# Three small edits to a fused attention and expert kernel: circuits mixed on TensorE, biases as bf16 parts, inverse norms as a power on GpSimd

## The reference

```python
q, k, v = split(query @ W_qkv.T + b_qkv)         # 8 heads of 16
encode(x) = x / max(sqrt(sum(x * x)), 1e-12) * exp(1j * phases)
q_ent, k_ent = entangle(encode(q)), entangle(encode(k))   # three depths
for c in range(4):                               # circuits
    scores = abs(pattern(q_ent, k_ent)) ** 2 * gain[c]    # 8 x 8 per token
    amps = sqrt(softmax(scores) + 1e-12)
    co = (amps @ vq) * coherence_phase
    final += sup_w[c] * clip(abs(co), 1e-6, 1.0) * sign(co)
attention = real(final) @ W_out.T + b_out
```

## Time and profile before

| | us |
|---|---|
| three runs of the kernel before | 1626.47, 1627.81 (median), 1628.41 |
| the profiled execution | 1626.89 |
| its span, from first to last instruction | 1624.8 |
| PE busy | 1261.8 (78%) |
| DVE busy | 1286.0 (79%) |
| ACT busy | 789.0 (49%) |
| POOL busy | 720.2 (44%) |

### The profile page before, as it was taken

One profiled execution on the slowest core, in us unless ns is written; L12 is line 12 of the kernel. 1 busy time (PEld: TensorE's weight loads), 2 busy tenths in 40 slices (PEclk: granted clock), 3 DMA queues, 4 the chain that ended last, 5 costly groups with the idle time before them and its releaser, 6 DMA issues.

```text
span 1624.8 us, 20010 instructions
## 1 busy us (share of the span) xinstructions
PE 1261.8 (78%) x6269; PEld 948.2 (58%) x6269; DVE 1286.0 (79%) x1606; ACT 789.0 (49%) x1605; POOL 720.2 (44%) x579
## 2 busy tenths in 40 slices
PE   4568988698987988698598988877888887988241
PEld 2345766667675666666377675746657574756131
DVE  6558788988969888888768898896788879888653
ACT  4337445545545554645436464543546465543110
POOL 1261423274534353475534352466625343435654
PEclk9989989889889979989788998979889899989575
DMA  7423321424323241523215141331515142331101
GB/s 210 132 71 96 100 80 55 125 72 118 101 61 105 63 134 52 164 72 116 74 49 163 40 149 48 100 99 57 169 36 157 39 135 76 97 82 34 33 20 45
DMA packets 110670, 147.27 MB, mean 91 GB/s; under 512 B 14921, under 2 KB 84198, under 8 KB 110054
## 3 DMA queue, kind: packets, MB, share of 16 engines
q1 hardware_dynamic: 101350, 125.01, 25.5%
q0 software_dynamic: 8192, 16.79, 3.3%
q10 hardware_dynamic: 1024, 4.20, 2.0%
HBM read 113.81 MB, written 32.13 MB: 90 GB/s over the span
## 4 chain that ended last, share of the span: by engine, by line
PE 47%; DVE 19%; ACT 13%; issue 11%; POOL 8%; DMA 1%; SPq 0%; ACTq 0%; POOLq 0%; DVEq 0%
PE ps_t L720 6%; PE ps_r L760 6%; PE ps_q L720 6%; PE ps_r L761 5%; PE ps_h L643 5%; PE ps_f L651 4%; DVE pat L1630 4%; POOL rows_in L1246 3%; DVE u_sgn L1704 3%; POOL got L1259 2%; DVE prod L1601 2%; PE ps_k L707 2%; PE ps_f L653 2%; ACT u_sgn L1066 2%; ACT hid L1085 2%
## 5 line engine op out<-in xcount | busy, mean ns | idle before, releaser
L1224 POOL TENSOR_TENSOR prod<-expo,vT 128x512 f32<-128x512 f32 x192 | 237.1, 1265 | 426.7 <-ACT expo L1048 265.1
L1216 POOL TENSOR_TENSOR prod<-kq 128x1024 f32<-128x1024 f32 x64 | 149.7, 2360 | 276.9 <-ACT kq L1020 276.9
L643 PE MATMUL ps_h<-turned,w_tile 128*128 128x128 f32 x1248 | 186.5, 296 | 65.8 <-ACT turned L1078 54.1
L643 PEld LDWEIGHTS ps_h<-turned,w_tile 128*128 128x128 f32 x1248 | 166.6, 204 | 109.0 <-ACT turned L1078 86.5
L1606 DVE TENSOR_TENSOR prod<-expo,ps_v 128x2048 f32<-128x2048 f32 x80 | 181.2, 2285 | 58.0 <-PE ps_t L720 35.2
L1630 DVE TENSOR_REDUCE pat<-prod 128x128 f32<-128x2048 f32 x96 | 218.7, 2280 | 9.7 <-POOL prod L1216 8.0
L1085 ACT ACTIVATE hid<-ps_h,w_tile 128x128 f32<-128x128 f32 x624 | 178.0, 368 | 64.8 <-PE ps_h L643 63.8
L1601 DVE TENSOR_TENSOR prod<-ps_q,kq 128x1024 f32<-128x1024 f32 x128 | 150.5, 1217 | 72.5 <-ACT kq L1020 59.0
L760 PE MATMUL ps_r<-sqx,mats 128*128 128x512 f32 x256 | 165.2, 732 | 49.7 <-ACT sqy L1000 31.6
L651 PE MATMUL ps_f<-w_tile,hid 128*128 128x128 f32 x1248 | 174.8, 286 | 2.3 <-ACT turned L1078 2.3
L1246 POOL DMA_INDIRECT rows_in<-xn,row_of x128 | 126.4, 987 | 87.9 <-DVE tile_expert L1590 50.1
(11 more groups left out here) (262 smaller groups left out, 2286.8 us busy)
## 6 DMA issues: line engine op xcount, KB each, us to landing
w_tile<-w_cat SPq DMA_DIRECT2D x156, 514.0 KB
x_tile<-rows_in SPq DMA_DIRECT2D x156, 64.0 KB
rows_out<-turned SPq DMA_DIRECT2D x156, 64.0 KB
rows_in<-u SPq DMA_DIRECT2D x2, 2496.0 KB, 11.7
yacc<-in_L_attn_query_dram SPq DMA_DIRECT2D x16, 256.0 KB, 4.0
out_dram<-yacc SPq DMA_DIRECT2D x16, 256.0 KB, 2.9
x_sb<-in_L_attn_query_dram SPq DMA_DIRECT2D x11, 256.0 KB, 4.0
b_tile<-in_L_ffn_b_dram SPq DMA_DIRECT2D x156, 0.5 KB
```

Of the source, the lines that this page charges most:

```text
L643: last = nc.tensor.matmul(ps_h[:, c, :], w_tile[:, n % WS, c * P:(c + 1) * P], turned[:, x_turn(n) % FS, 0, :], start=True, stop=True)
L1224: last = pool.tensor_tensor(dst[:, at], w[:, at], v[:, at], ALU.mult)
```

## The change

PE mixes the circuits: `clip_and_mix` ends with one product `u * u_sgn` over all 2048 values, and a new `mix_circuits` sums the four circuits with four f32 products by diagonal matrices that hold the weights. The sum lies in PSUM (`ps_t`), where `measure` reads it, so `sum_circuits` and `msum` go. `mix_circuits(o)` stands between `q_operands(k, 2)` and the tile before `control_tiles(n)`; in a routed step the wait for the routing's read of `ps_t` (`rank_read`) moves there with it. POOL inverts the norms in a new `invert_norms(n)`, the first call of its step: a lower limit and a power of -0.5. Both biases become three bf16 parts added in one pass: `b_out` through the 96-row product that `b_qkv` has, `b2` through a three-row product whose rows SP loads with each tile from a small table in DRAM.

```diff
-                sp.dma_start(b2_tile[:, n % WS, :], b2[bass.ds(e, 1), :]).then_inc(w_landed.of(n), 16)
+                sp.dma_start(b2_tile[:, n % WS, :], b2_parts[bass.ds(e, 1), :, :].rearrange("e r c -> (e r) c")).then_inc(w_landed.of(n), 16)
...
+            sp.wait_ge(bias_split, 12)
+            for part in range(3):
+                sp.dma_start(b2_parts[:, part, :], b_parts[32 * part:32 * part + E, QKV + C:QKV + 2 * C]).then_inc(cat_made, 16)
...
-                nc.tensor.matmul(ps_f[:, 1, :], ones[0:1, :], b2_tile[:, n % WS, :], start=False, stop=True).then_inc(turn_psum.sem, 1)
+                nc.tensor.matmul(ps_f[:, 1, :], ones_parts[:], b2_tile[:, n % WS, :], start=False, stop=True).then_inc(turn_psum.sem, 1)
...
+            def mix_circuits(k):
+                pe.wait_ge(mix_ready.sem, mix_ready.value(k))
+                for c in range(NC):
+                    last = nc.tensor.matmul(ps_t.rearrange("p (t c) -> p t c", t=T), sup_mats[:, c, :], u[:, :, c, :],
+                                            start=(c == 0), stop=(c == NC - 1))
+                last.then_inc(msum_psum.sem, 1)
...
-                    last = nc.tensor.matmul(ps_t[:, at], ones[0:1, :], b_out_row[:], start=False, stop=True)
+                    last = nc.tensor.matmul(ps_t[:, at], pick[:], b_parts[:, QKV:QKV + C], start=False, stop=True)
...
-            def norm_sqrt(k):
-                act.wait_ge(ss_step.sem, ss_step.value(k))
...
-                act.activation(norm[:], ss[:, 1, :], ACT.Sqrt).then_inc(norm_ready.sem, 1)
...
-            def sum_circuits(k):
...
-                    tt(msum[:], u_sgn[:, :, 0, :] if c == 1 else msum[:], u_sgn[:, :, c, :], ALU.add, msum_step)
+            def invert_norms(k):
+                pool.wait_ge(ss_summed.sem, ss_summed.value(k))
+                pool.tensor_scalar(ss[:, 1, :], ss[:, 0, :], 1e-24, None, ALU.max).then_inc(ss_clamped.sem, 1)
+                pool.wait_ge(ss_clamped.sem, ss_clamped.value(k))
                 if k >= 1:
-                    pool.wait_ge(meas_ready.sem, meas_ready.value(k - 1))
...
+                    pool.wait_ge(v_ready.sem, v_ready.value(k - 1))
+                tt(rnorm[:], ss[:, 1, :], minus_half[:], ALU.pow, rnorm_ready)
...
+                for c in range(NC):
+                    const(dve.tensor_scalar(sup_mats[:, c, :], ident[:], sup[:, c:c + 1], None, ALU.mult))
...
             def normalise(k):
-                dve.wait_ge(norm_ready.sem, norm_ready.value(k))
-                dve.tensor_scalar(rnorm[:], norm[:], 1e-12, None, ALU.max).then_inc(rnorm_step.sem, 1)
-                dve.wait_ge(rnorm_step.sem, rnorm_step.value(k, 1))
-                dve.reciprocal(rnorm[:], rnorm[:]).then_inc(rnorm_step.sem, 1)
-                dve.wait_ge(rnorm_step.sem, rnorm_step.value(k))
+                dve.wait_ge(rnorm_ready.sem, rnorm_ready.value(k))
...
-                for c in range(NC):
-                    dve.scalar_tensor_tensor(u_sgn[:, :, c, :], u[:, :, c, :], sup[:, c:c + 1], u_sgn[:, :, c, :],
-                                             ALU.mult, ALU.mult).then_inc(mix_ready.sem, 1)
+                tt(u[:], u[:], u_sgn[:], ALU.mult, mix_ready)
```

More of the change, by code:

```diff
@@ L179, in build @@
         w_gate = sb("w_gate", [P, E])
-        b_parts = sb("b_parts", [96, QKV], BF16)
+        b_parts = sb("b_parts", [96, QKV + 2 * C], BF16)
+        ones_parts = sb("ones_parts", [3, P], BF16)
         pick = sb("pick", [96, P], BF16)
@@ L219, in build @@
         ss = sb("ss", [P, 2, T * 3 * NH])
-        norm = sb("norm", [P, T * 3 * NH])
+        minus_half = sb("minus_half", [P, T * 3 * NH])
         rnorm = sb("rnorm", [P, T * 3 * NH])
@@ L346, in build @@
         sq_ready = signal("sq_ready", T)
-        ss_step = signal("ss_step", 2)
-        norm_ready = signal("norm_ready")
-        rnorm_step = signal("rnorm_step", 2)
+        ss_summed = signal("ss_summed")
+        ss_clamped = signal("ss_clamped")
+        rnorm_ready = signal("rnorm_ready")
         a0_ready = signal("a0_ready")
@@ L707, in project @@
                     nc.tensor.matmul(p_cols, xnT[:, k % XN, t * P:(t + 1) * P], w_proj[:], start=True, stop=False)
-                    nc.tensor.matmul(p_cols, pick[:], b_parts[:], start=False, stop=True).then_inc(proj_psum.sem, 1)
+                    nc.tensor.matmul(p_cols, pick[:], b_parts[:, 0:QKV], start=False, stop=True).then_inc(proj_psum.sem, 1)
             def sums(k, unit):
@@ L844, in _ @@
                     q_operands(k, 2)
+                if exists(o):
+                    if routed is not None:
+                        pe.wait_ge(rank_read.sem, rank_read.value(routed))
+                    mix_circuits(o)
                 tiles(k, 3, 4)
@@ L851, in _ @@
                 if exists(o):
-                    if routed is not None:
-                        pe.wait_ge(rank_read.sem, rank_read.value(routed))
                     turn_m(o)
@@ L1055, in abs_sign @@
                 if k >= 1:
-                    act.wait_ge(msum_step.sem, msum_step.value(k - 1))
+                    act.wait_ge(msum_psum.sem, msum_psum.value(k - 1))
                 else:
@@ L1195, in _ @@
             split(pool.memset(pick[:], 0.0))
+            split(pool.memset(ones_parts[:], 1.0))
             for row in (0, 32, 64):
                 split(pool.memset(pick[row:row + 1, :], 1.0))
-            pool.wait_ge(bias_in, 48)
+            split(pool.memset(minus_half[:], -0.5))
+            pool.wait_ge(bias_in, 80)
             split(pool.tensor_copy(b_parts[:], b_in))
@@ L1623, in sums @@
                     if k >= 1:
-                        dve.wait_ge(mix_ready.sem, mix_ready.value(k - 1))
+                        dve.wait_ge(msum_psum.sem, msum_psum.value(k - 1))
                     else:
@@ L1702, in clip_and_mix @@
                 dve.wait_ge(clip_ready.sem, clip_ready.value(k))
-                for c in range(NC):
-                    dve.scalar_tensor_tensor(u_sgn[:, :, c, :], u[:, :, c, :], sup[:, c:c + 1], u_sgn[:, :, c, :],
-                                             ALU.mult, ALU.mult).then_inc(mix_ready.sem, 1)
+                tt(u[:], u[:], u_sgn[:], ALU.mult, mix_ready)
             def measure(k):
-                dve.wait_ge(msum_step.sem, msum_step.value(k))
+                dve.wait_ge(msum_psum.sem, msum_psum.value(k))
                 dve.wait_ge(phase_ready.sem, phase_ready.value(k))
```

41 lines of the change are left out of this document (16 added, 25 removed).

## The result

The changed kernel takes 1702.9 us (median of 4 runs, 1697.4 to 1705.4) against 1628.1 us for the kernel before: a ratio of 1.0447, with a 95% interval from 1.0408 to 1.0485. That is 4.5% slower, where the prediction had 1577 us and a chance of 0.08 for slower. The profiled execution took 1697.4 us, its span 1695.7.

The account below looks back on a forecast made before the run. It took PE and DVE, handing work back and forth with neither full, to bound the kernel. Its terms, 24 + 5 + 2 - 5 + 6 + 2 + 16 = 50 us, took 1626.9 to 1577 us, range 1540 to 1610.

Parts of the forecast that it names:

- the price of the power: POOL's power of -0.5 on 96 values, at the head of its step: between 0.22 and 4.5 us, taken as 2 us.
- The rival that named the power: POOL's power is long: past 10 us each microsecond delays 15 steps, 1727 us at a 20 us power; chance 0.08.
- the room: At the head of POOL's step, read in block 7's step: the power may take about 10 us and cost nothing.
- the likeliest case: The forecast itself, 1577 us, with its own range 1562 to 1590 and chance 0.50.
- Mixing on PE: Four products after `q_operands`: 3.4 us at full clock, 6.8 at half; PE takes back all but 0.2 of DVE's 2.7 us.
- What the fill is worth: PE's 3.15 us idle before `measure` goes, full clock stays, DVE's 3.9 us of waits vanish: about 4 us a step.
- Rival 1: PE still falls to half clock after idling before `grow_once_more` and routed mixing; 1597 us, chance 0.20.
- Routed steps: Blocks 1, 5, 9: PE stands 6.4 us before mixing until DVE reads the ranks; still 0.7 us gained in each.
- Blocks 2 and 10: `target_tiles` ends no earlier than `measure` even before the change, so mixing adds to the path: 2.5 us lost in each.
- Step 15 and the end: POOL's gathers start earlier in step 15, 6.2 us gained; at the very end 0 to 4 us, taken as 2.
- Experts' bias: Three-row bf16 product saves 0.2 us in each of 156 tiles, 31 us of PE; half counted, 16 us.
- The output bias: Output projection's one-row bias costs 0.93 us a tile; with the 96-row bf16 form four tiles take 1.3 us, not 5.42.

## Why the prediction was wrong

**The step that failed** is the price of the power: "From above I take twenty times that, 4.5 us", and a value of 2 us, where it takes 15.69. The bound came from POOL's product, and a factor of twenty was put on it without a reason. Nothing in the trace showed the power or an operation that works like it, and a multiple of another operation's rate is no bound. The rival that named the power was given 0.08 on the argument that it "would have to cost 60 products a value". By the same reckoning (0.22 us for 96 products) it costs 71.

**A second step failed with it:** the room, "the power may take about 10 us and cost nothing". It was read in the step of block 7 and taken for all steps. With half the power, which ends inside that room, DVE waits in 3 of 16 steps, and the two steps before the first clip have no room: there the whole power delays the clip by 23 us, half of it by 11.7.

**The rival's mechanism was right and its price too low.** At 0.47 + 15.69 = 16.2 us its formula gives 1577 + 6.2 x 15 = 1670; measured are 1703. Its base, 1577, was 13 us too high beside the product's 1564, so its own term, 93 us, stands against 133. In block 7 the term holds: `measure` comes 6.6 us later than with the product in the power's place (22.9 against 16.3 us after the clip), the formula has 6.2. In block 8 the same distance is 9.4 us, as the power starts later against DVE's work there. The mean over the 14 distances from clip to clip is 7.9 us, and the 23 us before the first clip come on top. Among the 14 waits of the loop, block 7's 3.53 us is the third shortest. The prediction also said that the pattern product "has slack too"; it had, until the power was longer than that slack.

The Trainium skill (SBUF — State Buffer, Who interferes with whom) says that a DVE instruction with two SBUF inputs contends with a GpSimd instruction that reads SBUF, and calls the pair of ports that the two engines share an exclusive lock. For the pattern product the trace agrees: 3.37 us for `a` is close to one of POOL's two products (2.33, half of the 4.65 of the earlier trace rows) and `a`'s own 1.23, 3.56 together. For the power it does not. DVE's `u` by `u_sgn`, two SBUF inputs, took 2.29 us in the middle of the power's 15.69, in all 14 steps in which it lay there; that is also what it takes in the version with the old norms, where no power runs.

**The rest of the sum.**

- *Without the power's cost* the forecast was 1577 us. The kernel with a product in its place has 1563.9 us, the one with the old norms 1576.2. The nearer to what the prediction described is the first; it lies at the edge of the likeliest case's own range, 1562 to 1590. The sum itself, 50 us, is 11 us short of the 61 that this kernel gains, and that it came so near is in part luck: most of its terms missed, to both sides, as follows.
- *Mixing on PE.* Right: in the version with the old norms it takes 3.60 us in the step of block 7, close to the forecast (3.4), and PE goes from `target_tiles` straight into `turn_m`, with no wait for `measure`:

```profile
855.64 3.60 PE L732 MATMUL ps_t<-u,sup_mats 128*128 128x512 f32 x8
...
864.30 1.09 PE L766 MATMUL ps_r<-ident,a 128*128 128x128 f32 x8
865.23 0.60 PE L740 MATMUL ps_t<-ident,meas 128*128 128x128 f32 x4
...
870.06 1.12 PE L772 MATMUL ps_r<-sqx,mats 128*128 128x512 f32 x2 [1.27 <-ACT sqy L1009]
```

- *What the fill is worth.* Right in kind, low in size. That version's clock stays full, where the earlier trace rows had 0.50. From 19 to 29 us after the clip it is 1.00 in all 14 blocks, where the kernel before has 0.50 in seven of them and 0.60 to 0.90 in the rest. Rival 1's 2.4 us of idle in front of `grow_once_more` did come (2.40), yet the products behind it took 1.02 us, as at the full clock. Ahead of mixing in the routed steps the clock did fall as rival 1 had it (below). The stretch of block 7:

```profile
866.00:880.00 14.00, 10.25 (x43) 5.77 (x42) 13.86 (x20) 5.93 (x12) 4.66 (x2) 1.00 0.19 51
```

  DVE works 13.86 of these 14 us: the four waits of the earlier trace rows are gone, as forecast. From clip to clip blocks 0, 4, 7, 8, 11 and 13 take 5.4 to 8.2 us less; forecast were 4, and about 1 from the tiles. Blocks 3, 6 and 12 take 3.9 to 5.0 us less; forecast were 1.7, and the same 1. One reason: PE was to take back all but 0.2 us ahead of `spread`. With the product in the power's place `spread` of block 7 starts 18.4 us after the clip and in eight other blocks 16.6 to 17.0, where the kernel before has 19.1 to 19.5. The wait in front of `spread`, forecast at 2 to 3 us, is 1.5 at most outside the routed steps and block 10.
- *Routed steps.* Wrong in sign. Forecast were 0.7 us gained in each; with the old norms they grow by 2.2, 3.0 and 0.7 us. The idle time in front of mixing was foreseen (6.4 us; it is 7.75), but not that mixing behind it runs at the half clock, which rival 1 had: it takes 6.35 to 6.74 us in the three routed steps, behind 4.15 to 7.75 us of idle, and 3.60 elsewhere in the loop.
- *Blocks 2 and 10.* Forecast were 2.5 us lost in each: block 10 loses 2.9, block 2 gains 3.7.
- *Step 15 and the end.* Forecast 6 and 2 us; with the old norms 5.3 and 5.0.
- *Experts' bias.* Forecast 16 us, measured 16 (12 to 20) alone. A tile's bias takes 0.23 us instead of 0.49, so 0.26 us are saved where 0.2 was assumed; with half of it on the path that would be 20 us, so two small errors may have cancelled. The saving of 0.1 us by the rule of the Trainium skill (TensorEngine Tiling (Array Packing), Key Properties), which the prediction had weighed, did not come about.
- *The output bias.* The prediction took 0.43 us for a tile's product by `W_out` and left 0.93 for the one-row bias. The 0.43 is a step of the chain of waits, not the product. In the timeline of the kernel before the two take 0.72 and 0.73 us from start to start, at the half clock:

```profile
892.31 0.80 PE L735 MATMUL ps_t<-w_outT,measT 128*128 128x128 f32 x2
893.03 0.79 PE L736 MATMUL ps_t<-b_out_row,ones 1*128 1x128 f32 x2
893.76 0.80 PE L735 MATMUL ps_t<-w_outT,measT 128*128 128x128 f32 x2
```

  The sum does not suffer, as it went by the whole tile. But the prediction's comparison of 0.93 us with the 0.33 of the 96-row form set a half clock against a full one, so those two rows bear out nothing about the few-row form.

## What to carry to other kernels

The rate of one operation is no upper bound for another that no row shows. If the forecast breaks at some price (13.3 us here), not knowing the price is no ground for giving it a small chance. A run with that one instruction swapped for a product of the same shape tells what it costs. Room beside other work is to be read in several steps of the loop, the tightest above all and the first ones too, and together with the engine's next instruction behind the new one. A wait moved up an engine's queue takes along all that stands behind it: moving one call down again in three steps was worth 13 us or more.

## What the hardware showed that was not expected

- POOL's power of two f32 tensors: 15.69 us for 128 x 96 and 8.08 us for 128 x 48, against 0.39 us for a product of 128 x 96.
- The power does not hold up DVE. In 14 steps DVE's clip and its product of two SBUF operands lay wholly inside a power, and took 1.23 and 2.29 us each time. Beside POOL's ordinary products a DVE product of 1.23 us took 3.37 and one of 0.28 took 2.42, and the clip, which meets the pattern product in the version with the old norms, took 2.51 in block 7.
- A matrix product over three bf16 rows took 0.23 us a tile where the f32 one over a single row took 0.49 us.
